# Row maxima of two attention tiles: one VectorE instruction over two PSUM banks instead of two over one bank each

## The reference

```
x = x + 0.5 * ffn(layernorm(x), w_gate, w_up, w_down)       # silu(gate) * up, hidden 768, integer weights / 127
x = x + attention(layernorm(x), Wq, Wk, Wv, Wo, bo)         # 16 heads of 16, with ALiBi bias
x = x + 0.5 * ffn(layernorm(x), w_gate, w_up, w_down)

# attention, per sequence b and head h
scores = einsum('bhld,bhsd->bhls', qh, kh) * 16 ** -0.5 - slope[h] * abs(s - l)
attn   = softmax(scores, axis=-1)
out    = einsum('bhls,bhsd->bhld', attn, vh)                # then @ Wo.T + bo
```

## Time and profile before

| | |
|---|---|
| Three runs | 897.83, 895.79, 892.29 us; median 895.79 us |
| Profiled execution | 898.4 us, span 896.6 us |
| TensorE granted clock, mean | 0.966 of full |
| Busy in the span: PE, DVE, ACT, POOL | 92%, 72%, 58%, 48% |

### The profile page before, as it was taken

One profiled execution on the slowest core, in us unless ns is written; L12 is line 12 of the kernel. 1 busy time (PEld: TensorE's weight loads), 2 busy tenths in 40 slices (PEclk: granted clock), 3 DMA queues, 4 the chain that ended last, 5 costly groups with the idle time before them and its releaser, 6 DMA issues.

```text
span 896.6 us, 13035 instructions
## 1 busy us (share of the span) xinstructions
PE 825.1 (92%) x4576; PEld 503.3 (56%) x4576; DVE 647.6 (72%) x1359; ACT 522.5 (58%) x745; POOL 426.2 (48%) x486
## 2 busy tenths in 40 slices
PE   2999999858899999999999999999899987999997
PEld 2788888724354454453453444444443436888886
DVE  6898878567767777777777777776778715777764
ACT  4444434414667677777677677777577774344443
POOL 0444433422644654744644745645555545344443
PEclk9999999966999999999999999999799999999999
DMA  9320000283532532541531540540522000010001
GB/s 360 112 31 3 2 3 3 33 109 39 72 46 29 72 47 28 72 54 20 72 54 20 72 64 13 69 67 15 65 44 29 2 1 2 26 48 26 26 26 48
DMA packets 21491, 43.17 MB, mean 48 GB/s; under 512 B 3849, under 2 KB 5913, under 8 KB 21209
## 3 DMA queue, kind: packets, MB, share of 16 engines
q1 hardware_dynamic: 21400, 41.92, 27.3%
HBM read 12.02 MB, written 4.62 MB: 19 GB/s over the span
## 4 chain that ended last, share of the span: by engine, by line
PE 64%; DVE 21%; issue 4%; DMA 4%; ACT 3%; SPq 1%; POOL 1%; DVEq 0%; ACTq 0%
PE ps L938 60%; DVE row_max L859 7%; DVE hid L755 3%; DMA q_aug<-max_row 3%; PE ps L994 2%; ACT stage L612 2%; PE ps L950 1%; DVE xn L717 1%; DVE xnt L877 1%; DVE newton L694 1%; ACT xnt L618 1%; DVE var L686 1%; SPq L406 1%; DMA k_aug<-parts 1%; DVE mean_var L676 1%
## 5 line engine op out<-in xcount | busy, mean ns | idle before, releaser
L859 DVE TENSOR_REDUCE row_max<-ps 128x1 f32<-128x512 f32 x512 | 328.5, 684 | 117.6 <-PE ps L938 116.3
L650 ACT ACTIVATE probs<-ps 128x1024 f32<-128x1024 f32 x256 | 259.9, 1026 | 44.6 <-PE ps L938 44.1
L531 POOL TENSOR_TENSOR probs<-probs,diag 128x256 f32<-128x256 f32 x256 | 186.8, 734 | 199.3 <-ACT probs L650 199.1
L466 POOL TENSOR_TENSOR hid_r<-hid,hid_r 128x512 fp32r<-128x512 f32 x96 | 125.2, 1305 | 178.5 <-ACT hid_r L558 177.3
L938 PE MATMUL ps<-xnt,wgu_r 128*128 128x512 f32 x768 | 192.4, 406 | 12.1 <-DVE hid L755 7.9
L938 PE MATMUL ps<-k_aug,q_aug 60*128 60x512 f32 x512 | 171.4, 462 | 23.2 <-DVE row_max L859 10.6
L938 PEld LDWEIGHTS ps<-xnt,wgu_r 128*128 128x128 f32 x768 | 145.3, 193 | 54.0 <-DVE hid L755 14.9
L938 PE MATMUL ps<-probs,v_aug 128*32 128x512 f32 x1024 | 140.6, 622 | 6.9 <-POOL probs L531 6.9
L938 PE MATMUL ps<-q_aug,k_aug 62*128 62x512 f32 x512 | 130.9, 503 | 5.0 <-DMA q_aug<-max_row 4.6
L938 PEld LDWEIGHTS ps<-k_aug,q_aug 60*128 60x128 f32 x512 | 84.5, 195 | 81.2 <-DVE row_max L859 68.3
L564 ACT ACTIVATE gated<-ps 128x512 f32<-128x512 f32 x96 | 57.5, 599 | 121.0 <-PE ps L938 120.9
(11 more groups left out here) (63 smaller groups left out, 669.9 us busy)
## 6 DMA issues: line engine op xcount, KB each, us to landing
q_aug<-parts SPq DMA_DIRECT2D x96, 128.0 KB, 4.3
k_aug<-parts SPq DMA_DIRECT2D x96, 128.0 KB, 5.9
x_sb<-x_in SPq DMA_DIRECT2D x8, 512.0 KB, 12.8
x_out<-x_sb SPq DMA_DIRECT2D x8, 512.0 KB, 2.6
diag<-diag_table SPq DMA_DIRECT2D x1, 2048.0 KB, 18.9
wgu_i<-w_gate_up SPq DMA_DIRECT2D x2, 768.0 KB, 6.3
w_att<-w_att SPq DMA_DIRECT2D x1, 1024.0 KB, 11.7
q_aug<-max_row SPq DMA_DIRECT2D x64, 8.0 KB
```

The lines of the kernel that those rows point to most:

```text
L466: nc.gpsimd.tensor_tensor(hid_r[:, 1, f, :], hid[:, f % 2, :], hid_r[:, 0, f, :].bitcast(F32), ALU.subtract).then_inc(s["hid_lo"], 1)
L531: nc.gpsimd.tensor_tensor(tile, tile, diag[:, kt % 2, n * QH + 2 * pair:n * QH + 2 * pair + 2, :], ALU.mult).then_inc(fixed, 1)
L650: nc.scalar.activation(probs[:, kt % 2, 2 * pair:2 * pair + 2, :], ps[:, at:at + 2, :], ACT.Exp, scale=SLOPE_UNITS[pair]).then_inc(exp_don ...
L859: nc.vector.reduce_max(row_max[:, quad % 2, u % 2, u // STEPS, (u % STEPS) // 2:(u % STEPS) // 2 + 1], max_bank(b, tile)[0], mybir.AxisLis ...
```

## The change

The two tiles of a step are reduced by one instruction, [128, 2, 512] to [128, 2]. It waits until both products are done, and adds 2 to `s1_used`. Both products of a pair then wait until the joint maximum of the pair that used their banks has been read: the distance back is still 2 (or 4), counted from the pair's end. The four banks ahead of the loop are used pair by pair in the same order as before. The negation follows the same pair as before.

```diff
             if first(b) and tile < 2 * STEPS:
-                return ps[:, (4, 5, 2, 3)[tile % 4], :], 4
-            return ps[:, max_at + tile % 2, :], 2
+                return (max_at, 2)[tile // 2 % 2] + tile % 2, 4
+            return max_at + tile % 2, 2
...
-                for k in range(start, stop):
+                for k in range(start, stop, 2):
...
-                    dve.wait_ge(s1_done, b * MAX_TILES + tile + 1)
-                    nc.vector.reduce_max(row_max[:, quad % 2, u % 2, u // STEPS, (u % STEPS) // 2:(u % STEPS) // 2 + 1],
-                                         max_bank(b, tile)[0], mybir.AxisListType.X).then_inc(s1_used, 1)
-                    if u == 2 * STEPS - 1:
+                    at = max_bank(b, tile)[0]
+                    dve.wait_ge(s1_done, b * MAX_TILES + tile + 2)
+                    nc.vector.reduce_max(row_max[:, quad % 2, :, u // STEPS, u % STEPS // 2:u % STEPS // 2 + 1],
+                                         ps[:, at:at + 2, :], mybir.AxisListType.X).then_inc(s1_used, 2)
+                    if u == 2 * STEPS - 2:
                         negate(b * NQ + quad, quad % 2)
...
-                    wait(pe, s1_used, b * MAX_TILES + tile + 1 - back)
-                    matmul(bank, q_aug[seq % 2][rows:rows + ROW_MAX, pair, t * P:(t + 1) * P],
+                    wait(pe, s1_used, b * MAX_TILES + tile - tile % 2 + 2 - back)
+                    matmul(ps[:, bank, :], q_aug[seq % 2][rows:rows + ROW_MAX, pair, t * P:(t + 1) * P],
                            k_aug[seq % 2][rows:rows + ROW_MAX, pair, :], True, True).then_inc(s1_done, 1)
```

## The result

The changed kernel takes 914.6 us in the median (913.88 to 917.43, 4 runs), the kernel before 894.04 us beside it. The ratio is 1.0228 (95% interval 1.0198 to 1.0258): 2.3% slower, outside the range. The profiled execution took 917.43 us, 19.0 more than the 898.4 of the one before.

The account below looks back on a forecast made before the run. In plain odd steps the second maximum alone holds TensorE, by 0.1 us. -1.0 us per sequence over 7.4 sequences (-7.4) and +1.5 before the loop give -5.9 on 898.4: 892.5, as a median 890; range 878 to 911.

Parts of the forecast that it names:

- The instruction: Joint reduction on VectorE: 1.21 us for 1024 elements, so a pair's second maximum is there 0.08 us earlier.
- The wait on VectorE: The joint reduction waits for both products; where these run together it starts only 0.00 to 0.02 us later.
- The wait on TensorE: Both products wait until 1.27 us after the joint maximum starts, then go together and last 0.49 us.
- the odd steps: Eight steps per sequence with value products alone: pair to pair 1.80 us instead of 1.87; -0.62 us per sequence.
- rival A: Held pairs don't run together after a stall, 0.23 us each: 917 us, or 904 at half; chance 0.12.
- steps 4 and 5: Step with short heads transposes and the one after: -0.02 us over both, twice a sequence.
- quad 0: VectorE comes late and runs four maxima in a row; only the shorter reduction shows: -0.18 us per sequence.
- scores held by the transfer of the maxima: Sign of a wrong forecast: this transfer, which held scores for 0.41 us before, holds them in more quads.
- Quad 1: VectorE full, LayerNorm pieces between pairs: three reductions gain 0.08 us each, step 2 loses 0.05; -0.18 per sequence.
- Ahead of the loop: First 16 tiles gain 0.55 us; pairs then come every 2.10 us instead of 1.57, +2.1; together +1.5 us.
- B: Joint reduction not cheaper, or lost lead or 0.08 us more latency per wait: 901 or 911 us; chance 0.17.
- C: TensorE's granted clock: the change moves its rests, direction of the effect unknown, no size given; chance 0.08.

Follow-up runs that it names:

- late_start: The kernel before, but the first of a pair's two separate reductions waits for both products: 917.75 us, ratio 1.0244.
- one_count: The changed kernel, but only the second product of a pair raises the semaphore, once: 902.55 us, ratio 1.0079.
- kept_busy: The changed kernel with six more products, results overwritten, in step 4 of quad 1 where TensorE rests longest: 909.48 us, ratio 1.0181.

## Why the prediction was wrong

*The instruction.* Right: 1225 ns measured, 1.21 taken.

*The wait on VectorE*, "0.00 to 0.02 more". Wrong by a factor: the reduction starts 0.137 us after the pair, not 0.034 (medians over pairs that ran together, VectorE idle). late_start, whose reductions are single, has 0.068 with both increments awaited, 0.034 more than before; one_count puts the second increment by itself at 0.026. The other 0.07 comes with the form of the joint instruction: 0.137 against 0.068, with the same two increments awaited. The row of the scores pair and ScalarE said nothing about VectorE's form.

*The wait on TensorE and the odd steps.* The pair goes together, 0.49 to 0.50 long: right, and rival A is out. But the 0.10 above, with 0.02 more of the instruction, turned each plain odd step from -0.07 into +0.05 (1.92 against 1.87). The terms for steps 4 and 5 and for quad 0 lost their gain too. From scores to scores (medians of sequences 1 to 5) steps 4 and 5 of quads 2 and 3 take 4.05 us instead of 3.75, of which step 6 gives back 0.13; quad 0 takes 16.57 instead of 16.38, quad 2 16.41 instead of 16.14, and quad 3 is the same. These three had a gain in the forecast. That is the smaller failure: with the additions out of quad 1 the change costs 1.1% where the forecast had a gain of 0.7%. Of the signs, scores held by the transfer of the maxima did not come: those waits went from 13.7 and 4.6 us to 9.8 and 1.1.

*Quad 1*, -0.18 a sequence. This is the step that failed: the whole quad measured +2.4 (12.1/5). It took the durations of VectorE's pieces and of the negation as fixed. The rows of before spoke against that: the same instruction took 0.40 and 0.88 us in one quad 1, and 0.41 beside the 0.85 of the earlier trace rows in another; its mean of 598 ns hid two kinds. I read 0.85 as the instruction's cost, and half of it was a wait for GpSimd inside the instruction, which no view lists as a wait. With the additions moved away in both kernels quad 1 takes 16.54 us instead of 16.63: apart from the race, its term had the right sign. The traces show one instruction take 0.40 or 1.02 us by 0.03 us of order, with the long ones ending a fixed time behind GpSimd's (0.144 to 0.156 us). They show that the one waits; why it has to isn't shown.

*Ahead of the loop*, +1.5: from the first max product to the first scores it is +2.1; the period of the ten tiles on two banks, at a granted clock of 0.50 before and after, is 2.21 and not 2.10, by the same 0.10, and the first 16 tiles gain 0.40 and not 0.55.

*The rivals.* B had named 0.08 us more of latency in each wait as another way to 901 us (its terms add up to 900.4); the latency came, with 0.10. C was a part of it: in kept_busy quad 1 falls by 1.3 to 2.7 us when stretches of 3.4 to 6.8 us at a granted clock of 0.50 are kept at full, 0.3 to 0.4 us per us. Its chance was only 0.08, as I saw no reason why rests should lengthen. The rival that happened, a start 0.03 to 0.1 us later that loses a race against a GpSimd instruction and then the clock, was not on the list. Of the 2.3%, some 1.2 hang on GpSimd's additions in quad 1, races and clock together (1.1 is left when they stand elsewhere; one_count takes away 1.5, of which some 0.3 are its increments' own). The other 1.1 is the change's own price: the lost lead and the later start. How it divides between these two isn't shown, as their parts, measured apart, don't add up.

## What to carry to other kernels

Before costing a run of instructions on one engine as fixed, split a group whose durations come in two kinds (here 0.40 and 1.02 us): the longer kind may be a wait for another engine's instruction, and then a shift of a few hundredths of a microsecond, far below what a timed run can tell, can decide microseconds (here 0.026 us in one_count and 13 us). Two accesses to two buffers, joined to save time (here 1.29 to 1.23 us a pair), also join two waits; count what the earlier of the two had been hiding. When a small cause has a large effect, look for a threshold by shifting the start by hundredths and see which sequences flip.

## What the runs showed of the hardware

- A second semaphore increment at the end of a pair of products cost 0.026 us (0.137 us from the pair's end to the reduction with two, 0.111 with one).
- A joint reduction of two banks started some 0.07 us later after its semaphores than one over a single bank (0.137 against 0.068, two increments awaited in both), though it then lasted 1225 ns, 10 more than the line through 684 and 1746 gives. Why the start is later stays open.
- A wait of VectorE for GpSimd can lie inside an instruction's duration. A 128x256 LayerNorm piece took 0.40 us, or up to 1.44 us and then ended 0.15 us after a GpSimd instruction. Reductions that read PSUM showed no such kind: all 512 of the kernel before took 672 to 693 ns.
- TensorE's granted clock fell to half for 3.4 to 6.8 us in all five quads 1 looked at of the changed kernel, in or behind the rest of 1.71 to 1.72 us that each has (ahead of 376.04 above), and was at full in the four of kept_busy looked at, where that rest is filled. Before, it fell in two of five, though all five have the same longest rest, 0.66 to 0.68 us: such a rest alone doesn't decide it.
